# Node norms of a graph network: split parts ahead of the scaling, last tiles turned behind the next stage's first products, expert weights spread six products behind

## The reference

```python
logits = jnp.einsum('td,ed->te', xf, gate_w)
probs = jax.nn.softmax(logits, axis=-1)
top_w, top_i = jax.lax.top_k(probs, TOP_K)
top_w = top_w / (top_w.sum(axis=-1, keepdims=True) + 1e-09)
combine = jnp.zeros((T, N_EXPERTS), dtype=xf.dtype)
combine = combine.at[jnp.arange(T)[:, None], top_i].add(top_w)
h = jax.nn.gelu(jnp.einsum('td,edh->teh', xf, w1) + b1[None, :, :])
y = jnp.einsum('teh,ehd->ted', h, w2) + b2[None, :, :]
out = jnp.einsum('ted,te->td', y, combine)
```

## Time and profile before

| | |
|---|---|
| median of 3 runs | 1787.69 us (1787.13 to 1788.21) |
| the profiled execution | 1786.02 us, span 1784.2 us |
| TensorE busy (PE) | 1698.7 us, 95% of the span; mean granted clock 0.978 |
| VectorE (DVE), ScalarE (ACT), GpSimd (POOL) busy | 921.4 (52%), 453.9 (25%), 690.2 (39%) us |
| chain that ended last | PE 82%, DVE 8%, ACT 4% |

### The profile page before, as it was taken

One profiled execution on the slowest core, in us unless ns is written; L12 is line 12 of the kernel. 1 busy time (PEld: TensorE's weight loads), 2 busy tenths in 40 slices (PEclk: granted clock), 3 DMA queues, 4 the chain that ended last, 5 costly groups with the idle time before them and its releaser, 6 DMA issues.

```text
span 1784.2 us, 25791 instructions
## 1 busy us (share of the span) xinstructions
PE 1698.7 (95%) x10227; PEld 1588.6 (89%) x10227; DVE 921.4 (52%) x1892; ACT 453.9 (25%) x853; POOL 690.2 (39%) x428
## 2 busy tenths in 40 slices
PE   6799998999998988899899999999999999999999
PEld 6689998997998988889557789899999999998999
DVE  7984425616964759966567653533212132226541
ACT  3542313303122236934303321011011011112220
POOL 1026755562533631042020065443555335442564
PEclk9989999999998999899999999999999999999999
DMA  2001221244211210013010022111121112111222
GB/s 87 1 27 43 85 71 54 72 143 142 63 36 54 71 54 27 1 45 111 35 42 1 1 63 83 47 54 45 60 65 54 45 46 70 54 47 36 63 72 70
DMA packets 41999, 99.83 MB, mean 56 GB/s; under 512 B 10508, under 2 KB 12142, under 8 KB 41894
## 3 DMA queue, kind: packets, MB, share of 16 engines
q1 hardware_dynamic: 37828, 87.87, 16.1%
q10 hardware_dynamic: 4066, 10.46, 1.7%
HBM read 96.39 MB, written 1.92 MB: 55 GB/s over the span
## 4 chain that ended last, share of the span: by engine, by line
PE 82%; DVE 8%; ACT 4%; issue 1%; DVEq 0%; ACTq 0%
PE bank L2324 10%; PE bank L2326 10%; PE bank L2325 10%; PE banks L2324 9%; PE banks L2325 9%; PE banks L2326 9%; PE bank L2864 3%; PE banks L2864 3%; PE bank L2941 3%; PE bank L2946 3%; PE banks L2941 2%; PE banks L2946 2%; DVE edge_scores L1846 1%; PE bank L2560 1%; PE banks L2560 1%
## 5 line engine op out<-in xcount | busy, mean ns | idle before, releaser
L791 POOL TENSOR_TENSOR w_hi<-raw,ones_r 128x768 fp32r<-128x768 f32 (+1 forms) x192 | 294.1, 1532 | 1034.9 <-PE banks L2326 368.5
L794 POOL TENSOR_TENSOR w_lo<-raw,w_hi 128x768 fp32r<-128x768 f32 (+1 forms) x192 | 371.6, 1935 | 15.1
L2324 PE MATMUL bank<-w_hi,xT_hi 128*125 128x384 f32 (+2 forms) x560 | 188.3, 336 | 1.3 <-DVE small L1871 1.2
L2326 PE MATMUL bank<-w_hi,xT_lo 128*125 128x384 f32 (+2 forms) x560 | 187.4, 335 | 0.0
L2325 PE MATMUL bank<-w_lo,xT_hi 128*125 128x384 f32 (+2 forms) x560 | 187.3, 334 | 0.0
L2324 PE MATMUL banks<-w_hi,xT_hi 128*125 128x384 f32 (+2 forms) x440 | 151.7, 345 | 0.0
L2325 PE MATMUL banks<-w_lo,xT_hi 128*125 128x384 f32 (+2 forms) x440 | 151.4, 344 | 0.0
L2326 PE MATMUL banks<-w_hi,xT_lo 128*125 128x384 f32 (+2 forms) x440 | 151.3, 344 | 0.0
L2324 PEld LDWEIGHTS bank<-w_hi,xT_hi 128*125 128x125 f32 x560 | 104.7, 187 | 4.4 <-DVE small L1871 1.4
L2326 PEld LDWEIGHTS bank<-w_hi,xT_lo 128*125 128x125 f32 x560 | 104.6, 187 | 2.5
L2325 PEld LDWEIGHTS bank<-w_lo,xT_hi 128*125 128x125 f32 x560 | 104.6, 187 | 2.4
(11 more groups left out here) (565 smaller groups left out, 3936.5 us busy)
## 6 DMA issues: line engine op xcount, KB each, us to landing
raw<-wa SPq DMA_DIRECT2D x92, 384.0 KB, 3.1
raw<-wc SPq DMA_DIRECT2D x76, 384.0 KB, 3.0
raw<-wb SPq DMA_DIRECT2D x28, 448.0 KB, 3.3
w_rows<-w_in ACTq DMA_DIRECT2D x1, 3072.0 KB, 12.9
bias<-bias_in ACTq DMA_DIRECT2D x6, 384.0 KB
w_first<-w_in ACTq DMA_DIRECT2D x1, 2304.0 KB, 10.0
w_down<-w_down_in SPq DMA_DIRECT2D x8, 288.0 KB, 5.2
w_up<-w_up_in SPq DMA_DIRECT2D x1, 2304.0 KB, 11.4
```

What stands on the lines that cost most here:

```text
L791: pool.tensor_tensor(w_hi[:, k, 0:width], raw[:, k, 0:width], ones[:, 0:1].to_broadcast([P, width]), ALU.mult).then_inc(S("unit_high"), 1)
L794: pool.tensor_tensor(w_lo[:, k, 0:width], raw[:, k, 0:width], f(w_hi[:, k, 0:width]), ALU.subtract).then_inc(S("unit_split"), 1)
L2324: tell_used(pe.matmul(dst, l_hi, r_hi, start=start, stop=False))
L2326: return pe.matmul(dst, l_lo, r_hi, start=False, stop=stop)
```

## The change

Three things, in f0, f1, g2 and f3 (the norm in front of g1 keeps its order).

1. ROW_LAG = 2: VectorE splits tile n-2 between the statistics and the scaling of tile n; ScalarE rounds tile n-2 before the root and scaling of tile n.
2. `down` leaves the last `left` turns out (LEFT_TURNS). In f0, f1 and f3 tile 4 is turned behind the router's first half; the first job follows, then the router's second half, then job 1, then the turn of the logits. In g2 tiles 3 and 4 are turned behind tiles 0 and 1 of the first chunk of `g2a`. `plan_groups` follows.
3. EXPERT_LAG = 6: the spreading of the weights follows six jobs behind, the turning of `cpad` behind job 5, the wait for `cT` behind job 6; f1's importance sum goes behind job 3 (IMPORTANCE). TSLOTS stays 6.

```diff
@@ -78,8 +78,10 @@
 RING = 3
 TURN_LAG = 2
 LOW_LAG = 3
+ROW_LAG = 2
 SMALL = 608
-EXPERT_LAG = 5
+EXPERT_LAG = 6
+IMPORTANCE = 3
 ROWS_AT = {1: 0, 2: 1}
 SOURCES_AT = {3: (0, 1), 5: (2,), 7: (3,), 8: (4,), 10: (5,), 11: (6,), 13: (7,)}
 COLUMNS_AT, SHIFTS_AT, FIRST_SHIFT, NEXT_SHIFT = 4, 10, 11, 15
@@ -156,6 +158,9 @@
     return j // 2, j % 2
+LEFT_TURNS = {"f0": 1, "f1": 1, "f3": 1, "g2": TURN_LAG}
+
+
 def half_tiles(c):
     first = [(0, 0), (0, 1), (1, 0), (1, 1)] if c == 0 else [(0, 0), (1, 0), (0, 1), (1, 1)]
@@ -194,11 +200,21 @@
         several(following + "_xT", 2 * NT, following + "_xT_low")
         ends, turns = closing[plain:plain + NT], closing[plain + NT:]
         del closing[plain:]
-        for n in range(NT + TURN_LAG):
-            if n < NT:
-                closing.append(ends[n])
+        for n in range(NT):
+            closing.append(ends[n])
             if n >= TURN_LAG:
                 closing.extend(turns[2 * (n - TURN_LAG):2 * (n - TURN_LAG) + 2])
+        keep_turns(turns[2 * (NT - TURN_LAG):], following)
+
+    def keep_turns(turns, following):
+
+        later = 2 * LEFT_TURNS[following]
+        closing.extend(turns[:len(turns) - later])
+        left.extend(turns[len(turns) - later:])
+
+    def left_turn():
+        closing.extend(left[:2])
+        del left[:2]
     def several(label, n, sem, first=0, per=1):
         for i in range(n):
@@ -216,16 +232,19 @@
             add(label, i, label + "_settled", i + 1)
     def ffn(f, tiles):
-        several(f + "_routerT", 2, f + "_routerT_read")
+        add(f + "_routerT", 0, f + "_routerT_read", 1)
+        left_turn()
         jobs, lag = 2 * tiles, EXPERT_LAG
         for j in range(jobs + lag):
             if j < jobs:
                 add(f + "_hidden", j, f + "_activated", j + 1)
             if j == 0:
+                add(f + "_routerT", 1, f + "_routerT_read", 2)
+            if j == 1:
                 add(f + "_router", 0, f + "_routed", 1)
+            if j == IMPORTANCE and f == "f1":
+                add(f + "_importance", 0, f + "_importance_read", 1)
             if j == lag - 1:
-                if f == "f1":
-                    add(f + "_importance", 0, f + "_importance_read", 1)
                 several(f + "_cT", NT, f + "_combineT")
             if j >= lag:
                 add(f + "_cB", j - lag, f + "_weighted", j - lag + 1)
@@ -268,6 +287,8 @@
                 continue
             closing.append(("g2a", i))
             give_back("g2a", [i])
+            if i < TURN_LAG:
+                left_turn()
             if i in ROWS_AT:
                 add("g2p_rows", ROWS_AT[i], "g2p_rows_low", ROWS_AT[i] + 1)
             if i == min(SOURCES_AT):
@@ -356,7 +377,11 @@
                 if (r, c) == (RELS - 1, 1) and n >= TURN_LAG:
                     several_from(following, 2 * (n - TURN_LAG), 2, following + "_low")
         if key == "g3c":
+            plain = len(closing)
             several_from(following, 2 * (NT - TURN_LAG), 2 * TURN_LAG, following + "_low")
+            turns = closing[plain:]
+            del closing[plain:]
+            keep_turns(turns, "f3")
     ffn("f3", 12)
     return groups, where, {group: at for at, group in enumerate(closing)}
@@ -863,6 +888,8 @@
             def normal_rows(s):
                 for n in range(NT + TURN_LAG):
+                    if n >= TURN_LAG and s != "g1":
+                        tile_high(s + "_xT", KD, n - TURN_LAG)
                     if n < NT:
                         act.wait_ge(*E(s + "_aggregated", n + 1))
                         act.activation(rstd[0:TN, n:n + 1], moments[0:TN, 2 * n + 1:2 * n + 2], ACT.Sqrt,
@@ -873,8 +900,6 @@
                         if s == "g1":
                             act.wait_ge(*E("g1_xn", n + 1))
                             act.activation(nm_hi[:, n, 0:D], xn_g1[:, n], ACT.Copy).then_inc(S("g1_nodes_high"), 1)
-                    if n >= TURN_LAG and s != "g1":
-                        tile_high(s + "_xT", KD, n - TURN_LAG)
             def nodes_high(full, width, src, high, before=0):
@@ -1356,9 +1381,9 @@
                 def of(n):
                     measure(s, n)
+                    if n >= ROW_LAG:
+                        turned_low(s, n - ROW_LAG)
                     scale_rows(s, n)
-                    if n >= LOW_LAG:
-                        turned_low(s, n - LOW_LAG)
                 return of
             def node_tile(n):
@@ -1635,7 +1660,7 @@
                 dve.tensor_reduce(no_edge[0:TN], maskT[:], AX.X, ALU.max).then_inc(S("no_edge"), 1)
             def expert_layer(s, tiles, tile=None):
-                for n in range(NT - LOW_LAG, NT):
+                for n in range(NT - ROW_LAG, NT):
                     turned_low(s, n)
                 if s == "f3":
                     dve.memset(bias8[:], 0.0).then_inc(S("f3_rows_clear"), 1)
@@ -2364,7 +2389,7 @@
                     past[0] = True
             def down(key, label, lhs_hi, lhs_lo, ready, feed=0, seed=None, after=None, tile_ready=None, turn=None,
-                     beside=None):
+                     beside=None, left=0):
@@ -2408,7 +2433,7 @@
                             beside(c, k)
                     if after:
                         after(c)
-                for n in range(NT - TURN_LAG, NT):
+                for n in range(NT - TURN_LAG, NT - left):
                     if turn:
                         turn(n)
@@ -2470,7 +2495,9 @@
             def expert_layer(s, tiles, gate):
                 pe.wait_ge(*E(s + "_xT_pad", 2))
-                for c, (c0, cn) in enumerate(CH):
+
+                def router(c):
+                    c0, cn = CH[c]
                     pe.wait_ge(*E(s + "_xT_low", (6, 2 * NT)[c]))
                     dst = open_bank(s + "_routerT", c)
                     for k in range(KD):
@@ -2479,34 +2506,39 @@
                         last = pe.matmul(dst[0:2 * EXPERTS, 0:cn], gates[:, gate * KD + k].rearrange("p h e -> p (h e)"),
                                          xT_lo[:, k, c0:c0 + cn], start=False, stop=k == KD - 1)
                     close(last, s + "_routerT", c)
+
+                router(0)
+                turn_behind(s)(NT - 1)
                 jobs = 2 * tiles
                 for j in range(jobs + EXPERT_LAG):
                     if j < jobs:
                         up(s, j)
                     if j == 0:
+                        router(1)
+                    if j == 1:
                         pe.wait_ge(*E(s + "_routerT_read", 2))
                         dst = open_bank(s + "_router", 0)
                         for n in range(NT):
                             last = pe.transpose(dst[0:TN, 16 * n:16 * n + 16], router_T[:, n * TN:(n + 1) * TN],
                                                 ident[0:2 * EXPERTS, 0:2 * EXPERTS])
                         close(last, s + "_router", 0)
+                    if j == IMPORTANCE and s == "f1":
+                        pe.wait_ge(*E("f1_probs", 1))
+                        dst = open_bank("f1_importance", 0)
+                        for n in range(NT):
+                            last = pe.matmul(dst[0:TN, 0:8], ones[0:TN, 0:TN], prob8[0:TN, 8 * n:8 * n + 8],
+                                             start=n == 0, stop=n == NT - 1)
+                        close(last, "f1_importance", 0)
                     if j == EXPERT_LAG - 1:
-                        if s == "f1":
-                            pe.wait_ge(*E("f1_probs", 1))
-                            dst = open_bank("f1_importance", 0)
-                            for n in range(NT):
-                                last = pe.matmul(dst[0:TN, 0:8], ones[0:TN, 0:TN], prob8[0:TN, 8 * n:8 * n + 8],
-                                                 start=n == 0, stop=n == NT - 1)
-                            close(last, "f1_importance", 0)
                         pe.wait_ge(*E(s + "_combine", 4))
                         for n in range(NT):
                             dst = open_bank(s + "_cT", n)
                             close(pe.transpose(dst[:, 0:TN], cpad[:, n], ident[0:TN, 0:TN]), s + "_cT", n)
                         pe.wait_ge(*E(s + "_cT_pad", 1))
                         pe.wait_ge(*E(s + "_select", 4))
+                    if j >= EXPERT_LAG:
+
                         pe.wait_ge(*E(s + "_combineT", NT))
-                    if j >= EXPERT_LAG:
-
                         i = j - EXPERT_LAG
                         m, (c0, cn) = i // 2, CH[i % 2]
                         q, kind = (m // 3, m % 3) if tiles == 12 else (m // 2, 2 * (m % 2))
@@ -2524,7 +2556,7 @@
                                   start=True, stop=False)
                 down(s + "d", s + "_down", hT_hi, hT_lo, lambda k: pe.wait_ge(*E(s + "_low", 2 * k + 2)), seed=seed,
-                     turn=turn_behind("g2") if s == "f1" else None)
+                     turn=turn_behind("g2") if s == "f1" else None, left=LEFT_TURNS["g2"])
             pe.wait_ge(*E("consts", CONSTS))
@@ -2570,7 +2602,7 @@
```

(9 more changed lines are left out.)

## The result

The changed kernel takes 1774.32 us (median of 4 runs, 1773.27 to 1775.59), the kernel before in the same comparison 1787.95 (1787.13 to 1789.32): the ratio is 0.9928, with a 95% interval of 0.9916 to 0.9939, a difference of 13.6 us between the medians and of 11.9 between the two profiled spans. The forecast was 1776.2 with a range of 1767.5 to 1783.0.

A forecast was written before the change was run, and what follows sets the result against it. TensorE, busy 95% of the span, was taken as the bound. Wins of 19.8 us less losses of 8.3 gave net 11.5: 1786.02 to 1774.5, then 1776.2 us because the median lies 1.7 higher; range 1767.5 to 1783.

The forecast's parts named there:

- The order of the norms and the turned tiles: At the stage starts, earlier splits and later turns win 3.6 us in f0, 3.2 f1, 4.1 g2, 1.4 f3.
- the second rival: In f0 and f1, tile 3's scaling comes after GpSimd's next instruction begins; 6.2 us less in all, 1782; chance 0.17.
- The fourth rival: Starts of f0, f1 and f3 come no earlier, tile 2's split being late; 8.2 us less, 1784; chance 0.07.
- the middle of the bounds: At f3's start, the win was bounded by 0.8 and 1.9 us, depending on the low clock; 1.4 was taken.
- g2: At g2's start, a 2.5 us wait and a low-clock stretch go, a 0.5 wait comes; 4.1 us won.
- The spreading: In the expert jobs, waits for `cT` and `cpad` go: 0.9 us won in f0, 5.7 f1, 0.9 f3.
- f1's low clock: In f1's expert jobs, the lower clock from 561.78 to 567.2 goes with the `cpad` wait, worth 2.4 us.
- The ring of six: At the ends of jobs, activations wait for slots: 2.3 us lost in f0 and f3, 2.1 in f1, 6.8 together.
- The first rival: At the ends of jobs, no wait, as activation does not hang on the later broadcast; 1768 us; chance 0.13.
- the slower rival: Inside the expert run, the ring's delay reaches TensorE at a hidden product's bank; 26 us lost, 1802; chance 0.05.
- the 2.6 us: Inside the expert run, activation comes about 5.6 us after its product, its bank is wanted after 8.2: 2.6 to spare.
- I take one of three, 1.5: At the three ends of jobs, low clock costs 0 to 3 x 1.5 us; one fall, 1.5, was taken.

The follow-up runs named there:

- ring7: The changed kernel with a seventh slot for the activated tiles in f0, f1 and f3: 1765.02 us.
- swap: The changed kernel with VectorE's order turned round in the expert jobs, splitting job j-1 before weighing job j: 1770.83 us.
- lag5: The changed kernel with the expert lag back at 5, importance kept behind product 3: 1770.29 us.
- lag5_early: The changed kernel with expert lag 5 and the router's transposes right behind the router's second half, ahead of product 1: 1765.47 us.
- early_imp2: lag5_early with f1's importance sum behind product 2 instead of product 3: 1765.46 us.
- spread_alone: The kernel before with only the spreading part of the change (expert lag 6, importance behind product 3, later wait for the copies): 1787.06 us, ratio 1.0003.
- order_undone: The changed kernel with the old order of the norms, the turned tiles still behind the first products: 1792.97 us.
- turns_undone: The changed kernel with all tiles turned in front of the router and g2's first product again, new order of the norms kept: 1783.36 us.
- ring7_swap: The changed kernel with both the seventh slot and the turned VectorE order: 1770.13 us.
- early_imp2_ring7: early_imp2 with the seventh slot added: 1762.89 us.

## Why the prediction was right

**The order of the norms and the turned tiles.** Right in mechanism and nearly in size: 13.7 won against 12.3 forecast. The scaling operations of tiles 3 and 4 ended with GpSimd's first and third instruction (268.62 against 268.61, 271.95 against 271.93) and did not wait for the next, so the second rival did not come. By the Trainium skill (SBUF — State Buffer, section "Who interferes with whom") a VectorE instruction with two inputs in SBUF and a GpSimd instruction that reads SBUF shut each other out for the whole instruction. Both rows agree with it. The fourth rival (starts no earlier) falls with the router at 271.45. The router's first half started at 271.45 (forecast 271.5), tile 4 was turned at 273.16 (273.3). The two experiments on it show what the prediction did not say, that most of the win needs both halves. f3 was under-sized by 0.75: I took the middle of the bounds, and the low clock took 3.4 us instead of 6.8, so it came out above the upper one.

**g2.** 4.43 against 4.1; the wait for the second weight unit was 0.38 where 0.5 was forecast, and the clock stayed up.

**The spreading.** 8.4 against 7.5. The term that was too small is f1's low clock: the stretch from 560.5 to 567.5 cost about 3.0 us and not 2.4, since TensorE was at work in nearly all of it: 6.8 us at half speed, less the 0.7 of the wait for `cT` in it, halved. In f0 and f3 the spreading brought 0.2 more each.

**The ring of six.** Right, and shown by the seventh slot and the swap: waits of 1.17 and 0.96 against a forecast of 1.2 and 1.1, a down stage 3.55 us behind the last product against 3.4. The first rival (no wait) falls. Inside the run TensorE never waited for `tmp`, so the slower rival falls too; how much of the 2.6 us was to spare no run shows.

**The step that failed** is "I take one of three, 1.5": the clock fell at all three ends. The prediction counted the second down group's old wait (0.2 to 0.3, now gone) with the waits, the table has it with the clock. On the prediction's terms the waits cost 6.7 us against 6.8, and the falls of 3.4 us each cost 1.2 to 1.4, 3.9 in all against 1.5: the price of a fall was near, their number was wrong. The losses came to 10.6 where 8.3 was forecast, and the wins to 22.1 where 19.8 was: two errors of 2.3 us that cancel. Of the 1.9 us by which 1776.2 is off, 0.4 are the net and 1.5 are the medians: the execution of the kernel before lay 1.7 under its median, the changed kernel's only 0.2 under its own. The prediction's own range also has a slip: no low clock at the tails and f3 at its best give 1776.2 - 1.5 - 0.5 = 1774.2, not 1773.

**What it did not ask:** whether the lag pays for itself. It wins 8.4 us and loses 10.6. The forecast had the losses of one part beside its wins (7.5 against 8.3) and did not draw the conclusion, which lag5 shows: leaving the sixth product out wins 2.5 us by the marks, and the medians lie 4.0 apart. With the transposes done at once as well (lag5_early) the medians lie 8.9 apart; by the marks of the three stages 4.9 of this are the edit's, and the rest is the stretch from g2 to f3, f3's start and the time up to f0.

## What to carry to other kernels

A longer lag between a producer and its consumer needs as many more slots in the ring between them; where the ring doesn't grow, the run can hide it and the end of the run pays. The rows of ring7 suggest the same of PSUM banks, which no run here tests. Before the lag is lengthened to cover a late chain, look at where that chain starts: here moving five small transposes ahead of one product took away the wait for `cpad` in f0 and f3, and in f1 moving the importance sum one product forward as well did, without the lag's price at the ends. And when an instruction is put ahead on one engine to free a slot sooner, ask who waits for the one that it passed.

## What the runs showed of the hardware

The clock's falls are not settled by the length of a wait. From f0's norm on each lasted 3.4 or 6.8 us, but for the last of a run, which the program's end cuts short; ahead of f0's norm every run but early_imp2 has one of 13.7 us, near 90 us. The pair of waits of 1.1 to 1.2 and 0.9 to 1.0 us at the ends of jobs brought one in all three stages of the changed kernel, and in eight of nine in spread_alone, order_undone and turns_undone together, a single wait of 1.4 to 1.5 there (swap) in none; a wait of 1.8 to 2.0 for `cpad` in one of three in lag5, and in lag5_early's only one; the wait of 2.5 in front of g2's last turned tile in the kernel before and in turns_undone, not in spread_alone; the wait of 2.7 in front of f3's router, the same in all, in the changed kernel, in swap and in early_imp2, and not in ring7, ring7_swap, lag5, lag5_early and early_imp2_ring7.

The stretch from g2's score rows to f3's router, which but for the norm at its end no experiment touches, took from 986.1 us (ring7_swap) to 991.05 (spread_alone). Its length goes with the time that the clock was low in it: 23.9 us in the four kernels that took 986.1 to 986.6, 27.3 and 28.35 in those that took 987.5 and 988.35, 30.3 to 35.4 in the six that took 988.5 to 991.05. So a gain of 2 or 3 us ahead of such a stretch can be given back in it, as early_imp2 shows, and differences of that size between whole kernels say little about the edit unless the marks around the edit are read as well. Why the falls come where they do was not settled.
